# First attention: tokens stationary and probabilities moving, value weights applied to the sums

## The reference

```python
sa, ca, ga, ... = modulation rows, one row of 128 per batch
h = layernorm(x) * (1 + ca) + sa
Q = (h @ Wq.T).reshape(b, n, 8, 64);  K = (h @ Wk.T).reshape(b, n, 8, 64)
V = (h @ Wv.T).reshape(b, n, 8, 128)
attn = softmax(einsum('bnhr,bmhr->bhnm', Q, K))
x = x + ga * einsum('bhnm,bmhd->bnd', attn, V)
```

## Time and profile before

| | |
|---|---|
| median of 3 executions | 3649.86 us |
| the profiled execution's own time | 3650.1 us |
| its span (first to last instruction) | 3648.3 us |
| mean granted TensorE clock | 0.865 of full |
| first attention, from its first load to its last norm operation | 34.2 to 2016.6 us of the span |
| TensorE busy, 1000 to 1256 us | 254.21 of 256 us |
| VectorE busy, same window | 159.10 us |
| ScalarE busy, same window | 129.86 us |

### The profile page before, as it was taken

How to read it: one execution, slowest core, us unless ns; L and a number is a source line. 1 busy time by engine, 2 the same in 40 slices (tenths; PEclk the granted TensorE clock), 3 DMA queues, 4 the chain that set the end, 5 groups by cost and what they waited for, 6 DMA issues and landing times. The chain is left out here.

```text
span 3648.3 us, 66236 instructions
## 1 busy us (share of the span) xinstructions
PE 2904.6 (80%) x24092; PEld 2399.5 (66%) x24092; DVE 2667.7 (73%) x8520; ACT 1326.0 (36%) x2264; POOL 246.2 (7%) x155
## 2 busy tenths in 40 slices
PE   5999999999999999999999455656565656664455
PEld 2888888888888888888888344545454545442222
DVE  4565766756657566566664699999999999956775
ACT  2544454544545545455454022222222222211222
POOL 0000000000000000000000000000000000002220
PEclk8999999999999999999999667767676767666777
DMA  1000000000000000000000200000000000000000
GB/s 63 1 1 7 1 1 7 1 2 7 1 7 1 1 7 1 7 1 1 7 1 1 91 1 0 0 0 0 0 0 0 0 0 0 0 5 10 11 11 17
DMA packets 6553, 25.16 MB, mean 7 GB/s; under 512 B 1504, under 2 KB 2016, under 8 KB 5984
## 3 DMA queue, kind: packets, MB, share of 16 engines
q1 hardware_dynamic: 6368, 22.57, 1.6%
HBM read 14.18 MB, written 8.39 MB: 6 GB/s over the span
## 5 line engine op out<-in xcount | busy, mean ns | idle before, releaser
L605 PEld LDWEIGHTS obank<-v_one,probs 128*128 128x128 f32 x8192 | 1069.0, 190 | 91.2 <-issue 4.0
L605 PE MATMUL obank<-v_one,probs 128*128 128x129 f32 x8192 | 1078.6, 274 | 0.0
L352 ACT ACTIVATE probs<-bank 128x512 f32<-128x512 f32 x1024 | 583.8, 597 | 746.0 <-PE bank L593 448.7
L442 DVE TENSOR_REDUCE maxes<-ring 128x1 f32<-128x512 f32 x1024 | 659.9, 686 | 127.7 <-PE ring L573 104.9
L592 PE MATMUL bank<-q_hh,k_hl 128*128 128x512 f32 x1024 | 505.1, 493 | 2.6 <-issue 2.6
L593 PE MATMUL bank<-q_lm,k_h 65*128 65x512 f32 x1024 | 406.3, 397 | 0.0
L455 DVE RECIPROCAL recip<-obank 128x1 f32<-128x1 f32 x512 | 83.7, 164 | 414.4 <-PE obank L605 401.1
L573 PE MATMUL ring<-k_hl,q_hh 128*128 128x512 f32 x1024 | 338.0, 410 | 9.0 <-DVE k_hl L434 6.0
L1020 PE MATMUL ring<-ident_sb,to_turn 128*128 128x128 f32 x96 | 28.7, 437 | 377.7 <-ACT to_turn L856 367.8
L956 DVE TENSOR_TENSOR low_hot<-ids,low_iota 128x16384 f16<-128x16384 f16 x32 | 277.9, 8683 | 1.9 <-ACT ids L861 1.9
L1020 PEld LDWEIGHTS ring<-ident_sb,to_turn 128*128 128x128 f32 x96 | 16.1, 213 | 381.9 <-issue 348.6
(11 more groups left out here) (221 smaller groups left out, 3728.7 us busy)
## 6 DMA issues: line engine op xcount, KB each, us to landing
xt<-in_x SPq DMA_DIRECT2D x8, 512.0 KB, 9.1
out_x<-xt SPq DMA_DIRECT2D x8, 512.0 KB, 2.6
x<-out_x SPq DMA_DIRECT2D x1, 4096.0 KB, 12.2
out_x<-x SPq DMA_DIRECT2D x8, 512.0 KB, 2.6
pk_wq<-in_w_q SPq DMA_DIRECT2D x1, 1024.0 KB, 4.9
pk_wqT<-in_w_qT SPq DMA_DIRECT2D x1, 1024.0 KB, 6.9
wmod_sb<-in_wmod SPq DMA_DIRECT2D x2, 384.0 KB
w_qk_sb<-in_w_qk SPq DMA_DIRECT2D x1, 512.0 KB, 4.4
```

The source lines that it names most:

```text
L352: nc.scalar.activation(probs[:, half, i, :], st[s % 4], ACT.Exp).then_inc(st_free[s % 4], 1)
L442: nc.vector.tensor_reduce(maxes[:, i, k:k + 1], ring[bank_of(at)][:], AX.X, ALU.max).then_inc(rows_maxed, 1)
L605: mm = nc.tensor.matmul(obank[j % 2][:, 0:D + 1], probs[:, half, m, cols], v_one[h % 2][:, m, :], start=(m == 0), stop=(m == TB - 1))
```

## The change

- The product becomes `product` (one call per step, three steps behind the scores, LAG = 3): one float32 matmul with a 128x128 tile of normed tokens `x1` as stationary operand and 512 columns of `probs` moving; eight of them accumulate into `obank[half]`. There are 16 per head.
- `x1` is the layer-normed token without scale and shift, its last feature overwritten by 1.0. The normed tokens sum to zero over the features, so that the last one can be had from the others. `output_turns` makes, once, a matrix per batch (`turns_m`) that puts scale, shift and this repair on the value weights. GpSimd copies the matrix of a batch (`turn_of`) and the eight token tiles (`keys_of`) into the buffers in use.
- `v_of` goes. In its place `weights_of`, one float32 matmul of 128 columns per head, and ScalarE's `output_weights`, a copy of 128x128.
- ScalarE copies each 128x512 sum to SBUF (`sums_out`, after the exponentials of steps 3 and 11).
- TensorE then makes the outputs (`outputs`): four calls per head of two float32 matmuls of 129 columns, each call into one bank of the ring, in steps 13 and 14 of the head (`OUT_0`) and 5 and 6 of the next (`OUT_1`).
- `gather_output` takes both tiles of a bank: one reciprocal of 128x2 and two multiply-adds.
- The constants wait for the weights first, and the ring's order is written down anew.

```diff
+LAG = 3
+OUT_1, OUT_0 = (5, 6), (13, 14)
...
         def product_at(s):
-            if s >= 10:
-                return 0, 0, s - 10
-            return (1, 1, s - 2) if s >= 2 else (1, 0, s + 6)
+            return (1, s + 2 * TB - LAG) if s < LAG else (0, s - LAG)
...
             def iteration_uses(b, h):
...
+            for s in range(2 * TB):
+                if 3 <= s <= 10 and more:
+                    found += [("a", g + 1, s - 3, k) for k in range(2)]
+                if s in OUT_1 and g > 0:
+                    found += [("o", g - 1, 2 + OUT_1.index(s))]
+                if s == 11 and more:
+                    found += [("w", g + 1)]
+                if s == 12 and more:
+                    found += [("r", g + 1, k) for k in range(2)]
+                if s == 13 and h == H - 2 and not last:
+                    found += [("t", b + 1, k) for k in range(2)]
+                if s in OUT_0:
+                    found += [("o", g, OUT_0.index(s))]
...
+            if kind == "o":
+                return o_read, shift(b, 8 * n + 2 * uses[at][2] + 2, 8 * H)
```

GpSimd:

```diff
+            def turn_of(b):
+                nc.gpsimd.sem_inc(turns, 1)
+                nc.gpsimd.tensor_copy(turn_now[:], turns_m[:, bass.ds(b, 1), :].rearrange("p o d -> p (o d)")).then_inc(turn_ready, 1)
+
+            def keys_of(i):
+                nc.gpsimd.sem_inc(turns, 1)
+                nc.gpsimd.tensor_copy(x1[:, i, :], x1_next[:, i, :]).then_inc(x1_ready, 1)
```

ScalarE:

```diff
+            def output_weights(b, h):
+                if not (isinstance(b, int) and b * H + h < 2):
+                    wait_full(b, located(b, "o", h - 2, 3))
+                at = located(b, "w", h)
+                wait_full(b, at)
+                nc.scalar.activation(w_out[h % 2][:, 0:D], ring[bank_of(at)][:, 0:D], ACT.Copy).then_inc(w_ready, 1)
+
+            def sums_out(b, h, half):
                 g = b * H + h
...
+                if not (isinstance(g, int) and g == 0):
+                    wait_full(b, located(b, "o", h - 1, 2 * half + 1))
+                act.wait_ge(product_done, 2 * TB * g + TB * half + TB)
+                nc.scalar.activation(sums[half][:], obank[half][:], ACT.Copy).then_inc(sum_read, 1)
...
-                if i == 0 and not (isinstance(b, int) and g == 0):
-                    act.wait_ge(o_full[1], 2 * (2 * g + half) - 2)
+                if s % 4 == 0 and not (isinstance(b, int) and g == 0):
+                    act.wait_ge(product_done, 2 * TB * (g - 1) + s + 4)
...
                         exponentials(b, h, s)
+                        if s == 3 and not (first and h == 0):
+                            sums_out(b, h - 1, 1)
+                        if s == 11:
+                            sums_out(b, h, 0)
```

VectorE:

```diff
+            def output_turns(link):
+
+
+                last = ident[:, P - 1:P]
+                diag = spread(ident[:], 1, B)
+                link(nc.vector.tensor_tensor(acc[:], diag, mod[:, 0], ALU.mult))
+                link(nc.vector.tensor_reduce(shift_col[:, 0, :], acc[:], AX.X, ALU.add))
+                link(nc.vector.tensor_scalar(shift_col[:, 1, :], mod[:, 1, :, D - 1], last, -1.0, ALU.mult, ALU.mult))
+                link(nc.vector.tensor_tensor(turns_m[:], diag, mod[:, 1], ALU.mult))
+                link(nc.vector.tensor_tensor(turns_m[:, :, 0:D - 1], turns_m[:, :, 0:D - 1], spread(shift_col[:, 1, :], 2, D - 1), ALU.add))
+                nc.vector.tensor_copy(turns_m[:, :, D - 1], shift_col[:, 0, :]).then_inc(turns_made, 1)
...
+            def gather_output(link, b, h, c):
+
+
+                g, at = b * H + h, located(b, "o", h, c)
+                wait_full(b, at)
+                o = ring[bank_of(at)][:, 0:2 * (D + 1)].rearrange("p (j d) -> p j d", j=2)
+                link(nc.vector.reciprocal(recip[:, 2 * c:2 * c + 2], o[:, :, D]))
+                if h % H != 0:
+                    dve.wait_ge(o_read, 8 * (g - 1) + 2 * c + 3)
+                for j in range(2):
+                    t = 2 * c + j
+                    if h % H == 0:
+                        nc.vector.tensor_scalar(acc[:, t, :], o[:, j, 0:D], recip[:, t:t + 1], None, ALU.mult).then_inc(o_read, 1)
+                    else:
+                        nc.vector.scalar_tensor_tensor(acc[:, t, :], o[:, j, 0:D], recip[:, t:t + 1], acc[:, t, :], ALU.mult, ALU.add).then_inc(o_read, 1)
```

In VectorE's `body` the call stands behind `row_maxima` of the same step, and ahead of the norm operation:

```diff
+                        if s in OUT_1 and not (first and h == 0):
+                            gather_output(link, b, h - 1, 2 + OUT_1.index(s))
+                        if s in OUT_0:
+                            gather_output(link, b, h, OUT_0.index(s))
```

TensorE; in its `body` the order of a step is scores, score_rows, product, outputs of `OUT_1`, weights_of, turn_max, turn_h, outputs of `OUT_0`:

```diff
+            def weights_of(b, h):
+                at = located(b, "w", h)
+                bank = take(b, at)
+                if h % H == 0:
+                    pe.wait_ge(turn_ready, b + h // H + 1)
+                give(at, nc.tensor.matmul(bank[:, 0:D], turn_now[:], wv_sb[:, h % H, :], start=True, stop=True))
...
+            def product(b, h, s):
+                g, half, i = b * H + h, s // TB, s % TB
+                pe.wait_ge(st_free[s % 4], 4 * g + s // 4 + 2)
+                if i == 0 and not (isinstance(g, int) and g == 0):
+                    pe.wait_ge(sum_read, 2 * g + half - 1)
+                if h == 0 and half == 0:
+                    pe.wait_ge(x1_ready, TB * b + i + 1)
+                nc.tensor.matmul(obank[half][:], x1[:, i, :], probs[:, half, i, :], start=(i == 0), stop=(i == TB - 1)).then_inc(product_done, 1)
+
+            def outputs(b, h, c):
+                g, half = b * H + h, c // 2
+                at = located(b, "o", h, c)
+                bank = take(b, at)
+                if c % 2 == 0:
+                    pe.wait_ge(sum_read, 2 * g + half + 1)
+                    pe.wait_ge(w_ready, g + 2)
+                for j in range(2):
+                    cols = slice((2 * (c % 2) + j) * P, (2 * (c % 2) + j + 1) * P)
+                    mm = nc.tensor.matmul(bank[:, j * (D + 1):(j + 1) * (D + 1)], sums[half][:, cols], w_out[h % 2][:], start=True, stop=True)
+                give(at, mm)
```

More of the change, by code:

```diff
@@ L158, in build_attention @@
         k_h1 = [sb(f"k_h1{i}", [R + 1, N], F32R) for i in range(2)]
-        v_one = [sb(f"v_one{i}", [P, TB, D + 1]) for i in range(2)]
+        turns_m = sb("turns_m", [P, B, P])
+        turn_now = sb("turn_now", [P, P])
+        shift_col = sb("shift_col", [P, 2, B])
+        x1_next = sb("x1_next", [P, TB, D])
+        x1 = sb("x1", [P, TB, D])
+        w_out = [sb(f"w_out{i}", [P, D + 1]) for i in range(2)]
+        sums = [sb(f"sums{i}", [P, HALF]) for i in range(2)]
         maxes = sb("maxes", [P, TB, 2])
@@ L192, in build_attention @@
         turns = sem("turns")
-        primed = [hT_ready, lo_ready, v_ready, rows_maxed, neg_ready, *st_free, *o_read]
+        primed = [hT_ready, lo_ready, w_ready, rows_maxed, neg_ready, *st_free, o_read]
         def iteration_uses(b, h):
             g, last = b * H + h, b == B - 1
+            more = not (last and h == H - 1)
             found = []
[L200 to L204, removed]
+            for s in range(2 * TB):
[11 more added lines that the diff above has]
+                    found += [("o", g, OUT_0.index(s))]
             if not (last and h >= H - 2):
@@ L297, in body @@
                             second_k(g + 1, h + 1)
+                        if s == 5 and h == H - 1 and not last:
+                            pool.wait_ge(ring_full[bank_of(located(b, "w", h))], filled(b, located(b, "w", h)))
+                            turn_of(b + 1)
+                        behind, at = product_at(s)
+                        if at >= TB and ((h == H - 1 and not behind and not last) or (h == 0 and behind and not first)):
+                            now = b if behind else b + 1
+                            if at == TB:
+                                pool.wait_ge(x1_made, now + 1)
+                            pool.wait_ge(product_done, (now * H - 1) * 2 * TB + at + 1)
+                            keys_of(at - TB)
                         if not first and h == 2 and s == 1:
@@ L304, in _ @@
             second_k(0, 0)
+            pool.wait_ge(turns_made, 1)
+            turn_of(0)
+            pool.wait_ge(x1_made, 1)
+            for i in range(TB):
+                keys_of(i)
             batches(pool, body)
@@ L374, in _ @@
             batches(act, body)
+            sums_out(B - 1, H - 1, 1)
         @block.vector
@@ L419, in first_norm @@
             def first_norm(link, n, b, count):
-                norm_step(link, n, tiles_of(b), h_tok[:], row(1, b), row(0, b), count, h_ready)
+                norm_step(link, n, tiles_of(b), h_tok[:], row(1, b), row(0, b), count, h_ready, keep=True)
             def second_norm(link, n, b, count):
@@ L449, in whole_max @@
                 nc.vector.tensor_tensor(row_max[:], maxes[:, :, 0], maxes[:, :, 1], ALU.max).then_inc(max_ready, 1)
[L451 to L461, removed]
+            def gather_output(link, b, h, c):
[11 more added lines that the diff above has]
```

(23 more changed lines are left out.)

76 lines of the change are left out of this document (29 added, 47 removed).

## The result

The median went from 3649.4 us (3648.41 to 3650.11) to **3710.7 us** (3707.41 to 3710.84, four executions each). The ratio is 1.0169, 95% interval 1.0157 to 1.0181: slower by 61 us. The profiled execution took 3710.74 us, its span is 3708.9 (3650.1 and 3648.3 before).

A forecast was written before the change was run, and what follows sets the result against it. TensorE's instruction stream was taken as the bound. The terms summed to +0.92 us a head, times 62 = +57, with +3 at the ends +60 on 3650.1: 3710 us, range 3660 to 3748.

The forecast's parts named there:

- Product: TensorE's 16 products a head, two wide passes each: 13.73 us against 14.24, -0.5 us a head.
- Values and outputs: On TensorE, per head: v_of goes, -1.79 us; weights_of +0.22; outputs +1.79; together +0.22.
- Start of a head: First pass of q and k to first product: steps shorten, the wait for VectorE's k_hl grows, +0.1 us a head.
- The new wait: Second row matmul of steps 6 and 7 waits some 0.55 us for a gather's ring bank: +1.1 us a head.
- Once a batch: Head 0's values wait less for the residual, -0.08 us a head; head 6's first output waits for turned tokens, +0.06.
- Ends: Outside the 62 heads: output_turns +5.5 us, first values -2, head 0's rows phase +3, tail -3.3; together +3.
- the free ring: Rival at the second row matmul of steps 6 and 7: bank free in time, -68 us, 3642; chance 0.11.
- half a wait: Rival at the ring: releases or reads are quicker, waits of 0.28 us each, 3676 us; chance 0.12.
- VectorE's lateness at the head's end: Rival before the low parts: 0.3 us margin used up by one norm operation, +34 us, 3744; chance 0.14.
- Weight loads as the limit: Rival in the product: loads bind, a wide pass could cost 0.235 us, -387 us, 3323; chance 0.03.
- signs named beforehand: Profile after: wide passes 0.43 us apart, steps 1.33 and 1.80, load idle 0.5 twice a head, head 30.9, TensorE busy -3%.

The follow-up runs named there:

- narrow: own01 with each product cut into four matmuls of 128 columns with the same stationary tile: 3662.1 us, ratio 1.0038.
- own01: The changed kernel with all outputs, of both halves, in the product's own banks and not in the ring: 3631.3 us, ratio 0.9953.
- own1: The changed kernel with the outputs of steps 5 and 6 in obank[1] and not in the ring: 3642.1 us, ratio 0.9983.
- late_out: The changed kernel with the outputs of steps 5 and 6 in steps 9 and 10, the residual moved from step 9 to 10: 3675.7 us, ratio 1.0075.
- own0: The changed kernel with the outputs of steps 13 and 14 in obank[0] and not in the ring: 3700.2 us, ratio 1.0142.
- turns_late: The changed kernel with output_turns behind the first norm, nothing else: 3704.7 us, ratio 1.0153.

## Why the prediction was right

It said 3710 and slower, and 3710.7 was measured. The mechanism that decides the sign was forecast and is shown; that the number fits to a microsecond is luck. Step by step:

- **Product.** Forecast 1.33 and 1.80 us a step, measured 1.32 and 1.78. The forecast rounded: eight narrow passes are 8 x 0.1117 = 0.894, less 0.858 is 0.036 a step and 0.57 a head, where the sum took 0.03 and 0.48. narrow supports the reason: eight passes in place of two, of the same columns, cost 31 us, with all eight loads beside them.
- **Values and outputs.** Shown as a sum only, with the product: own01's head is 0.33 us shorter than before; the stated terms without the ring waits and head 6 (-0.48, -1.57, +1.79, +0.1, -0.08) make -0.24, and -0.33 with 0.57 in place of 0.48. No run takes the terms apart. Of the 20.7 us that own01 gains over the 62 heads, 8.8 fall in the seven intervals that hold head 0 of a batch, where the residual's wait shrank, and 0.22 a head in the others.
- **Start of a head.** The interval stays fixed, 6.86 us in the changed kernel (q and k's first pass at 1044.20, first product behind the rows at 1051.06), 6.87 in the earlier trace rows.
- **The new wait.** Forecast 0.55 twice a head, read as 0.55 in the timeline inside the loop. own1's head takes (1958.11 - 104.83) / 62 = 29.89 us, 1.15 less than the changed kernel's: 0.57 each. One of two taken away (late_out) gives 35 us, both (own1) 69. This is the step that decides the sign, and it is shown. Its price isn't the same everywhere: from head 2 to head 7 of a batch a head is 0.96 us longer than in own1 in the two batches outside the loop (30.36 against 29.40) and 1.25 in the six inside (30.67 against 29.43). Two waits of 0.47 and of 0.55 make 0.94 and 1.10; most of the rest lies on the way from the product ahead of the first output to the row matmul behind it: 1.89 us inside the loop (1022.25 to 1024.14), 1.77 in batch 0 and 1.76 in own1. Why the ring costs more inside the loop no run shows.
- **Once a batch.** Head 6's wait was there with 0.6 us of gap (0.5 forecast), and some 0.8 us by the intervals of own0. The residual's wait fell from 1.2 to 0.4 us of gap, 0.8 where 0.7 was forecast. late_out took the rest away.
- **Ends.** Start +6.9 where 6.5 was forecast (output_turns 5.5 of it; turns_late moved head 1's maximum by 6.5 and the median by 6.0), tail -3.6 where 3.3 was.
- **What I missed** is the turn of the loop. It was in no term of the sum. Of the changed kernel's gaps before the first scores of a batch 10.2 us are in five turns, against 2.6 in the kernel before: +7.6 in gaps, 6.6 by the intervals of own0.

How it came out, over the 62 heads of the profiles: the outputs of steps 5 and 6 cost 71.2 us (own1; 68.2 forecast), those of 13 and 14 with the turns 10.0 (own0; 3.7 forecast, head 6's wait alone), both taken out together 0.6 more than singly, and what is left is 20.7 below the kernel before (own01; 14.9 forecast). That makes 61.1 where 57 was forecast, 4 us too little. The ends were forecast at 3 and measured at 3.3. The rest of the kernel, whose code is unchanged, happened to take 3.8 less in the changed kernel's profile than in the one before; it took 1627.8 to 1631.0 in the eight experiments. So the 4 us were made good by a difference that nobody could forecast.

The rivals: the free ring is refuted by the gap between the two row matmuls of L647, 0.69 us where 0.235 is usual (1056.52 to 1057.21); half a wait by late_out and own1. VectorE's lateness at the head's end didn't come: its low parts still follow ScalarE at once, and inside the loop the heads with norm operations and those without take the same 30.64 to 30.70 us. Weight loads as the limit fell by narrow, where four times as many cost 31 us and not hundreds. In that rival the prediction says that 1.6 times the narrow pass would put a product a little over a third of its price; by its rows it is 1.6 x 0.1117 = 0.18 of 0.429, or 0.42. The measured 0.43 a pass decides against it either way. Of the signs named beforehand, TensorE's busy time in the window fell by 2.2% (some 3% forecast), and the idle time of the second row matmul's load is 0.73 us (0.5).

## What to carry to other kernels

Before routing a result through a shared pair of banks, write down the order of uses and ask for each what TensorE has to do between filling the bank and needing it again: here 0.70 us of work stood against 1.25 us of gather, and the engine without slack paid the difference 124 times. A bank that its owner leaves empty at that moment (the product's own) showed no wait of its own here and turned a loss of 61 us into a gain of 17, and of 22 with output_turns moved. Wider moving operands brought little here (31 us of 3631 for float32), where passes already followed each other at the price of their columns; compute the price per column from two rows before expecting anything of the width.

## What was not expected of the hardware

The end of a loop turn can be dear on TensorE. The trace before, from the first pass of q and k to the next batch's first scores, 2.37 us with four passes of 0.43 between them:

```profile
1039.05 1.88 PE L555 MATMUL ring<-hT,w_qk_sb 128*128 128x512 f32 x4
...
1041.42 0.50 PE L592 MATMUL bank<-q_hh,k_hl 128*128 128x512 f32 x1 [0.48 <-issue]
```

and the changed kernel, 3.64 us:

```profile
1074.43 0.19 PEld L631 LDWEIGHTS ring<-hT,w_qk_sb 128*128 128x128 f32 x1 [0.24 <-DVE acc L538]
1074.86 1.88 PE L631 MATMUL ring<-hT,w_qk_sb 128*128 128x512 f32 x4
...
1078.50 0.49 PE L666 MATMUL bank<-q_hh,k_hl 128*128 128x512 f32 x1 [1.76 <-issue]
```

"Issue" means that the trace shows nothing that it waited for. In the changed kernel q and k take a bank that a gather released shortly before. My reading, which no run shows directly, is that TensorE's instruction stream can't run ahead into the next turn then, and the jump and the new instructions lie open. What is shown is that the dearer turn comes from having the outputs of steps 13 and 14 in the ring, where q and k wait for their gather: with the outputs of steps 13 and 14 out of the ring (own0) the five gaps shrink to 1.7 us, and with only those of steps 5 and 6 out (own1) they stay at 10.9. What the roughly 4 us between the last wait and the next turn's first matmul consist of isn't shown by any run. narrow, with many more instructions a turn, has gaps of 7.5 us in ten places there though no gather is in the ring; that was not looked into further. The price of a turn isn't steady either: the five intervals with a turn took 34.6, 34.6, 34.9, 35.1 and 36.7 us in the changed kernel, and 33.6 to 33.9 (three) and 35.3 us (two) in own1.
